# Moving the start-up loads and scale chains of a graph layer with expert routing, and its bias from a matmul to a vector add

## Chip, cores and metric

The kernel runs on one core of a Trainium2 chip. The metric is the device time of one execution in microseconds (us), the median over the runs.

## What is computed

The input is x (6250 nodes, 512 features, float32), a list of 106,250 edges sorted by destination, and the weights of one graph layer and of one layer of 16 experts. Cut to what matters:

```python
def _L0_gnn_ref(x, src, dst, W_self, b_self, W_neigh, gamma, beta, alpha):
    deg = segment_sum(ones_like(src), dst, N)
    agg = segment_sum(x[src], dst, N)
    neigh = agg * (1.0 / maximum(deg, 1.0))[:, None]
    h = x @ W_self + b_self + neigh @ W_neigh
    h = layernorm(h) * gamma + beta
    h = where(h >= 0, h, alpha * h)
    return h + x
x = x + _L0_gnn_ref(_layernorm(x), src, dst, ...)
x = x + _L0_ffn_ref(_layernorm(x), gate_weight, w1, w2)   # top 2 of 16 experts, mean over each expert's tokens
```

## The kernel before

Nodes are worked in 49 tiles of 128 (the last, the tail, has 106). All matmuls of float32 data are made of two float16 parts of each operand, a high and a low one: `split_mm` issues three products for each of four chunks, 12 matmuls in all.

**Stage one, tiles in order.** SyncE loads x tiles into a ring of eight (`load_x`). VectorE takes their statistics (`stats_of`), four tiles form a quarter, and `scales_of(q)` turns the quarter's means and variances into the scale and bias of the normalization. For quarters 0 and 1 all of that is on VectorE; from quarter 2 on VectorE only aggregates (counter `a_mv`) and GpSimd computes the chain (counter `a_stat`). ScalarE normalizes (`normal`), TensorE transposes (`turn_x`), ScalarE casts the high part and VectorE subtracts for the low one (`turned_high`, `turned_low`), and TensorE multiplies by the neighbour weights (`project`, through `split_mm`). The result is stored as a table row pair of float16 (`neigh_high`, `neigh_low`, `store_table`). The instruction order on ScalarE is written out by hand: for each tile i the cast of tile i, the normalization of i+2, the high part of the projection of i-1. Between tiles VectorE and TensorE do side work given by tables of tile numbers (`lists`): the edge lists (`passed_tiles` at tile 1, `turns`, `hits` and so on), and at tiles 17 to 25 the maxima of the self weights (`self_maxima`), their scale (`powers`), the bias parts (`self_bias`) and low parts (`self_low`).

The neighbour weights are scaled by a power of two drawn from their largest magnitude (`powers(1, 7, 0, 1)`), then cast in one ScalarE instruction (line 684) and lowered in one VectorE instruction (line 1300). All weights are loaded from ScalarE's queue in the first microseconds, the edge lists and then x from SyncE's.

**Stage two, edges in order.** The edges are cut into 208 groups of 4 x 128. For each, GpSimd issues four indirect gathers of 128 table rows (2 KB each) into a ring of four groups (line 617); it reuses a place in the ring when TensorE's step counter `c_step` says that the group is spent. A step (`step`) multiplies one-hot matrices made by ScalarE with the gathered rows and adds into one of two PSUM banks; there are 257 steps, one more at each tile's border. Beside the first 45 steps TensorE also computes one tile's self product each (`side`): a bias matmul of `kilo` and `bparts` (line 934), then 12 products; four more of these stand ahead of them. When a tile's steps are done, VectorE evicts it in `gnn`: it scales and adds the self product (line 1344), clears the bank, which frees it for TensorE (line 1346), then takes the moments, normalizes, applies the slope, adds the residual, and normalizes again into two float16 halves (lines 1349 to 1369). In 16 of the tiles it also takes a maximum of expert weights, and in 16 others it splits them (lines 1379 and 1382).

**Stage three** routes tokens on VectorE, gathers them by expert, runs the experts, and mixes and stores the output.

## Time and profile before

| | |
|---|---|
| median of three timed runs | 1692.03 us (1685.09 to 1693.57) |
| the profiled execution's own time | 1686.77 us |
| its span, first to last instruction | 1685.0 us |
| mean granted TensorE clock | 0.887 of full speed |
| TensorE matmuls busy | 1217.9 us (72%) |
| VectorE busy | 1028.5 us (61%) |
| GpSimd busy | 992.6 us (59%) |
| ScalarE busy | 886.9 us (53%) |

The busy shares are averages over stages with different limits, so they don't say what an edit is worth: that is read from the stage in which the edited work runs. A line number such as L617 is that of the kernel before; PE is TensorE, PEld its weight load, DVE VectorE, ACT ScalarE, POOL GpSimd, SP SyncE. A number in brackets behind an instruction is how long its engine stood idle before it, and what ended that.

### The profile page before, as it was taken

What the parts mean: (1) busy time and instruction counts of PE and PEld (TensorE: products, weight loads), DVE (VectorE), ACT (ScalarE), POOL (GpSimd) and SP (SyncE); (2) the same over time, 40 slices, a digit from 0 to 9 for tenths busy, and PEclk for the clock granted to TensorE, in tenths of its full rate; (3) what the DMA queues carried; (4) which work ended last, traced back from release to release, by engine and by line L of the source; (5) the groups of instructions that cost most, each with busy time, mean ns of one, the idle gap of its engine ahead of it and who ended that gap; (6) DMA issues with size and microseconds to landing.
All of it is one profiled execution on the core that took longest, in us unless ns stands there. A gap on an engine that the chain in (4) does not pass through costs nothing.

```text
span 1685.0 us, 37100 instructions
## 1 busy us (share of the span) xinstructions
PE 1217.9 (72%) x7688; PEld 644.5 (38%) x7696; DVE 1028.5 (61%) x2918; ACT 886.9 (53%) x1932; POOL 992.6 (59%) x1193
## 2 busy tenths in 40 slices
PE   4989899999665555665565546666677159999876
PEld 2545444444322222222222222234444146777612
DVE  6676235546666665657566655655658966666626
ACT  3455445555644444444444444446667838888402
POOL 2223277676777777777777777777776025555200
PEclk9999999999988888778878897799999669999885
DMA  5445277777888887888888888778877526666547
GB/s 194 141 139 166 108 219 252 243 250 225 265 265 268 264 245 237 280 260 296 261 281 279 285 279 275 240 237 249 246 233 219 216 80 201 199 200 205 192 167 275
DMA packets 141638, 384.99 MB, mean 228 GB/s; under 512 B 22911, under 2 KB 23041, under 8 KB 141509
## 3 DMA queue, kind: packets, MB, share of 16 engines
q0 software_dynamic: 75840, 248.18, 48.9%
q1 hardware_dynamic: 62392, 130.43, 21.8%
q10 hardware_dynamic: 3276, 4.97, 0.9%
q8 instruction: 43, 0.70, 0.2%
q14 instruction: 87, 0.70, 0.1%
...
## 4 chain that ended last, share of the span: by engine, by line
PE 39%; POOL 24%; issue 16%; DVE 9%; DMA 7%; POOLq 2%; SPq 2%; ACT 1%; DVEq 0%; ACTq 0%
POOL work L617 24%; PE ps L861 13%; PE ps L960 10%; PE ps L1053 6%; DMA work<-table,work 4%; PE ps L1064 3%; PE ps L1055 3%; POOLq L612 2%; PE ps L1113 1%; SPq L525 1%; DMA work<-in_w_t 1%; DMA work<-in_x 1%; PE ps L907 1%; DVE slots L1515 1%; PE ps L934 1%
## 5 line engine op out<-in xcount | busy, mean ns | idle before, releaser
L617 POOL DMA_INDIRECT work<-table,work x832 | 828.4, 996 | 295.6 <-issue 239.8
L960 PE MATMUL ps<-work 128*128 x2056 | 574.6, 431 | 345.0 <-DMA work<-table,work 329.5
L960 PEld LDWEIGHTS ps<-work 128*128 128x128 f16 x2056 | 216.4, 106 | 589.9 <-issue 445.3
L715 ACT ACTIVATE work<-work,ones 128x512 f16<-128x512 f16 x259 | 185.3, 715 | 325.7 <-PE ps L963 325.2
L709 ACT ACTIVATE work<-iota_row,work 128x128 f16<-128x128 f32 x1040 | 331.3, 390 | 31.6 <-ACT work L715 23.9
L861 PE MATMUL ps<-wparts,slots 128*128 128x512 f16 x1176 | 274.1, 383 | 12.2 <-DVE slots L1251 12.2
L1339 DVE TENSOR_SCALAR inv<-ps 128x1 f32 (+2 forms) x49 | 7.7, 158 | 336.6 <-PE ps L963 331.9
L633 POOL DMA_INDIRECT slots<-x_d,betab x114 | 107.8, 946 | 161.8 <-PE ps L1064 83.9
L861 PEld LDWEIGHTS ps<-wparts,slots 128*128 128x128 f16 x1176 | 115.8, 99 | 139.8 <-DVE slots L1251 14.7
L1053 PE MATMUL ps<-work,wparts 128*128 x456 | 156.1, 382 | 2.2 <-ACT wparts L801 2.0
L801 ACT COPY wparts<-ps 128x1024 f16<-128x1024 f16 x114 | 115.3, 1012 | 59.8 <-PE ps L1064 59.1
L1055 PE MATMUL ps<-work,wparts 128*128 x456 | 125.0, 274 | 0.0
L1553 DVE TENSOR_REDUCE work<-ps 128x256 f32<-128x512 f32 x114 | 78.7, 691 | 41.4 <-PE ps L1055 40.3
L963 PEld LDWEIGHTS ps<-onesh,work 128*128 128x128 f16 x1028 | 68.3, 102 | 76.5 <-issue 28.5
L729 ACT COPY wparts<-ps 128x1024 f16<-128x1024 f16 (+1 forms) x49 | 49.4, 1009 | 81.3 <-PE ps L976 80.2
L721 ACT ACTIVATE slots<-ps,wscale 128x512 f32<-128x512 f32 (+1 forms) x49 | 33.6, 686 | 103.0 <-PE ps L861 103.0
L1545 DVE TENSOR_TENSOR slots<-slots,work 128x256 f32 x114 | 52.8, 464 | 39.2 <-issue 24.5
L1064 PE MATMUL ps<-identh,slots 128*128 128x128 f16 x912 | 70.8, 221 | 5.1 <-DMA slots<-x_d,betab 5.1
L1064 PEld LDWEIGHTS ps<-identh,slots 128*128 128x128 f16 x912 | 61.4, 99 | 20.3 <-issue 5.3
L681 ACT ACTIVATE work<-ps 128x512 f16<-128x512 f32 (+1 forms) x49 | 29.2, 596 | 75.7 <-PE ps L861 75.7
L587 POOL TENSOR_SCALAR var<-mv 128x4 f32<-128x4 f32 x11 | 2.5, 228 | 108.3 <-DVE mv L1233 108.3
L963 PE MATMUL ps<-onesh,work 128*128 128x1 f16 x1028 | 64.1, 166 | 0.0
...
## 6 DMA issues: line engine op xcount, KB each, us to landing
...
```

The costliest lines, as they stand in the source:

```text
L617: pool.indirect_dma_start(out=gath[:, g % GRING, w, :], out_offset=None, in_=table[:, :], in_offset=bass.IndirectOffsetOnAxis(ap=idx_all[: ...
L633: pool.indirect_dma_start(out=xf[:, b, :], out_offset=None, in_=x2_d[:, :], in_offset=bass.IndirectOffsetOnAxis(ap=idx2[:, k:k + 1], axis= ...
L709: last = act.activation(away[:, par, w, :], iota_row[:, :], ACT.Abs, bias=negd[:, ds(GT * k + w, 1)])
L715: act.activation(hot[:, slot, :, :], away[:, slot % 2, :, :], ACT.Relu, bias=ones[:, 0:1], scale=-1.0).then_inc(c_hot, 1)
L801: act.copy(xft[:, b, :, :, :], chunks16(bank16(6 + n % 2), P)).then_inc(f_xt, 1)
L861: last = pe.matmul(to, left(a, c), right(w, c), start=start and c == 0 and a == 0 and w == 0, stop=c == n - 1 and a == 1)
L960: pe.matmul(ps[:, ds(bank, 1), :], hot[:, s, w, :], gath_row[:, ds(at + (2 * w + half) * D, D)].unsqueeze(1), start=False, stop=True, skip ...
L963: last = pe.matmul(ps[:, BANKS:2 * BANKS, 0:1][:, ds(bank, 1), 0], hot[:, s, w, :], onesh[:, :], start=False, stop=True, skip_group_check= ...
L1053: pe.matmul(ps[:, HBANK + b, :].rearrange("p (u a n) -> p u a n", u=1, a=2), xft[:, b, 0, c, :], both, start=c == 0, stop=c == CHUNKS - 1, ...
L1055: last = pe.matmul(ps[:, HBANK + b, FF:2 * FF].unsqueeze(1), xft[:, b, 1, c, :], high, start=False, stop=c == CHUNKS - 1, skip_group_check ...
L1064: last = pe.transpose(bank16(6 + n % 2)[:, j * P:(j + 1) * P], xf[:, b, j * P:(j + 1) * P], identh[:, :])
L1553: dve.tensor_reduce(hid[:, b, :], ps[:, HBANK + b, :].rearrange("p (a n) -> p n a", a=2), X, ALU.add).then_inc(f_pre, 1)
```

## The change

1. SyncE issues the first four x tiles ahead of the edge lists. VectorE takes their statistics before it turns to the neighbour weights, and quarters 0 and 1 get their scale chain on GpSimd as the others do.
2. The six loads that are not the neighbour weights (self and gate weights, bias, alpha, gamma, beta) move from ScalarE's queue to GpSimd's, behind the scale chain of quarter 0. The four spare fills and the store to the first row of x2 now stand behind them.
3. ScalarE normalizes tiles 0 and 1 before it casts the neighbour weights, and casts them in four chunks; VectorE lowers each chunk as it comes, and the first projection waits chunk by chunk.
4. The bias matmul of each self product goes, with the bias's maximum and its preparation in two float16 parts. VectorE adds the float32 bias to each finished tile in `gnn`, behind the clear that frees the bank and ahead of the moments.
5. The bias stays in SBUF for longer, at a place that expert 14's weights take later; so expert 14's load moves from the first group of the last loads to the late one, which then has four loads instead of three.

```diff
@@ -185,11 +183,12 @@
         xin = cut(UNROLL * D, 0).rearrange("p (b n) -> p b n", b=UNROLL)
         xs = cut(HALF * D).rearrange("p (b n) -> p b n", b=HALF)
         tb = cut(HALF * D).bitcast(f16).rearrange("p (b n) -> p b n", b=HALF)
-        RAW_AT = place[0]
+        BSELF_AT = 14464
         wst = cut((2 * D + EXPERTS) * CHUNKS)
         ws, wn, gw = (wst[:, a * CHUNKS:b * CHUNKS].rearrange("p (c n) -> p c n", c=CHUNKS)
                       for a, b in ((0, D), (D, 2 * D), (2 * D, 2 * D + EXPERTS)))
-        bself = cut(D)
+        assert place[0] <= BSELF_AT
+        bself = cut(D, BSELF_AT)
         TABLES = GROUPS * GT + (STEPS + 3) * GT + STEPS + GROUP_CHUNKS * P + TILES
         assert place[0] <= WORK - TABLES
         idx_all = cut(GROUPS * GT, WORK - TABLES).bitcast(i32)
...
@@ -373,6 +369,14 @@
                 sp.sem_inc(d_st[b], 16)
             sp.sem_inc(v_st, 16)
             sp.sem_inc(d_x2st, 16)
+            def load_x(i):
+                r = rows_of(i)
+                if i >= UNROLL:
+                    sp.wait_ge(a_xs, i - UNROLL + 1)
+                sp.dma_start(xin[0:r, i % UNROLL, :], x[i * P:i * P + r, :]).then_inc(a_x[i % UNROLL], 16)
+
+            for i in range(HALF):
+                load_x(i)
             early = (GROUP_CHUNKS - 1) * P * GE_EDGES
             whole = (EDGES - early) // GE_EDGES
             half = whole - whole % 16
@@ -389,18 +393,12 @@
                              a[early + whole * GE_EDGES:EDGES].rearrange("(p e) -> p e", p=1)).then_inc(s_edge, 16)
 
 
-            def load_x(i):
-                r = rows_of(i)
-                if i >= UNROLL:
-                    sp.wait_ge(a_xs, i - UNROLL + 1)
-                sp.dma_start(xin[0:r, i % UNROLL, :], x[i * P:i * P + r, :]).then_inc(a_x[i % UNROLL], 16)
-
             def store_table(i):
                 r = rows_of(i)
                 sp.wait_ge(a_z, i + 1)
                 sp.dma_start(table[i * P:i * P + r, :], tb[0:r, i % HALF, :]).then_inc(a_st[i % HALF], 16)
 
-            for i in range(UNROLL):
+            for i in range(HALF, UNROLL):
                 load_x(i)
             for i in range(TILES + 2):
                 if i + UNROLL < TILES:
...
@@ -485,13 +483,13 @@
             sp.wait_ge(c_step, HOTS + STEPS)
             sp.wait_ge(c_away, STEPS + 3)
             sp.wait_ge(c_hot, STEPS + 2)
-            for e in list(range(9)) + list(range(12, EXPERTS)):
+            for e in list(range(9)) + [12, 13, 15]:
                 load_w1s(e)
             store_x1(LAST, 0, TAIL)
             store_x2(LAST, 0, TAIL)
             for b in range(2):
                 sp.wait_ge(d_st[b], 16 * (1 + len(range(b, TILES, 2))))
-            for e in range(9, 12):
+            for e in (9, 10, 11, 14):
                 load_w1s(e)
 
             def load_x1(i, rows):
...
@@ -572,18 +569,12 @@
                                base=-1, pattern=[[1, EXPERTS + 1]], channel_multiplier=-1).then_inc(s_const, 1)
 
 
-            pool.wait_ge(s_const, 2)
-            for n, s in enumerate(c_g):
-                pool.dma_start(spare[16 * n:16 * (n + 1), :],
-                               zero[16 * n:16 * (n + 1), :].bitcast(f16)).then_inc(s, 16 * GT)
-            pool.dma_start(x2_d[0:1, :], zero[0:1, :].bitcast(f16)).then_inc(d_zero, 16)
-
             def scales_of(q):
                 tiles = part_tiles(q)
                 n, r, c0 = len(tiles), slice(0, rows_of(tiles[-1])), q % 2 * HALF
                 at, c = slice(q * HALF, q * HALF + n), slice(c0, c0 + n)
                 v, g, f = (a[:, HALF:2 * HALF] for a in (var, guess, fix))
-                pool.wait_ge(a_mv, q - 1)
+                pool.wait_ge(a_mv, q + 1)
                 ln.link(pool.tensor_scalar(v, mv[:, c0:c0 + HALF, 1], EPS, None, ALU.add))
                 ln.link(pool.tensor_scalar(g.bitcast(i32), v.bitcast(i32), -0.5, float(0x5f3759df), ALU.mult, ALU.add))
                 for _ in range(3):
@@ -594,11 +585,26 @@
                 pool.tensor_scalar(rstd1[r, at], g[r, 0:n], 1.0, None, ALU.add)
                 ln.link(pool.tensor_tensor(nmr[r, at], mv[r, c, 0], g[r, 0:n], ALU.mult))
                 ln.link(pool.tensor_scalar(nmr[r, at], nmr[r, at], -1.0, None, ALU.mult))
-                pool.wait_ge(a_xs, HALF * (q - 1))
+                if q >= 2:
+                    pool.wait_ge(a_xs, HALF * (q - 1))
                 pool.tensor_scalar(gs[r, c], g[r, 0:n], SCALE, None, ALU.mult)
                 pool.tensor_scalar(gb[r, c], nmr[r, at], SCALE, None, ALU.mult).then_inc(a_stat, 1)
 
-            for q in range(2, PARTS):
+            scales_of(0)
+
+            for to, what in ((ws[:, :, :], w_self.rearrange("(c p) n -> p c n", p=P)),
+                             (gw[:, :, :], gate_t.rearrange("(c p) n -> p c n", p=P)),
+                             (bself[:, :], b_self.to_broadcast([P, D])), (alphab[:, :], alpha.to_broadcast([P, 1])),
+                             (gammab[:, :], gamma.to_broadcast([P, D])), (betab[:, :], beta.to_broadcast([P, D]))):
+                pool.dma_start(to, what).then_inc(s_w, 16)
+
+            pool.wait_ge(s_const, 2)
+            for n, s in enumerate(c_g):
+                pool.dma_start(spare[16 * n:16 * (n + 1), :],
+                               zero[16 * n:16 * (n + 1), :].bitcast(f16)).then_inc(s, 16 * GT)
+            pool.dma_start(x2_d[0:1, :], zero[0:1, :].bitcast(f16)).then_inc(d_zero, 16)
+
+            for q in range(1, PARTS):
                 scales_of(q)
 
             for b in range(HALF):
@@ -650,11 +656,6 @@
             act.sem_inc(g_rts, CREDIT)
             act.sem_inc(c_self, 2)
             act.dma_start(wn[:, :, :], w_neigh.rearrange("(c p) n -> p c n", p=P)).then_inc(s_wn, 16)
-            for to, what in ((ws[:, :, :], w_self.rearrange("(c p) n -> p c n", p=P)),
-                             (gw[:, :, :], gate_t.rearrange("(c p) n -> p c n", p=P)),
-                             (bself[:, :], b_self.to_broadcast([P, D])), (alphab[:, :], alpha.to_broadcast([P, 1])),
-                             (gammab[:, :], gamma.to_broadcast([P, D])), (betab[:, :], beta.to_broadcast([P, D]))):
-                act.dma_start(to, what).then_inc(s_w, 16)
 
 
             def normal(i):
@@ -680,10 +681,11 @@
                     act.wait_ge(a_st[i % HALF], 16 * (i // HALF))
                 act.activation(tb[0:r, i % HALF, 0:D], ps[0:r, 2 + i % 2, :], ACT.Copy, scale=2.0 ** -ZBITS).then_inc(a_zhi, 1)
 
-            act.wait_ge(w_scale, 1)
-            act.activation(wnp[:, 0, :, :], wn[:, :, :], ACT.Copy, scale=wscale[:, 0:1]).then_inc(w_hi, 1)
             normal(0)
             normal(1)
+            act.wait_ge(w_scale, 1)
+            for c in range(CHUNKS):
+                act.activation(wnp[:, 0, c, :], wn[:, c, :], ACT.Copy, scale=wscale[:, 0:1]).then_inc(w_hi, 1)
             for i in range(TILES):
                 if i == TILES - LIST_TILES:
                     act.wait_ge(b_done, 1)
@@ -912,13 +914,17 @@
                 pe.wait_ge(a_lo, i + 1)
                 if i >= 2:
                     pe.wait_ge(a_z, i - 1)
-                split_mm(ps[0:r, 2 + i % 2, :], lambda a, c: xt[:, i, a, c, 0:r], lambda w, c: wnp[:, w, c, :],
-                         CHUNKS).then_inc(a_mm, 1)
+
+                def weights(w, c):
+                    if i == 0 and w == 0:
+                        pe.wait_ge(w_lo, c + 1)
+                    return wnp[:, w, c, :]
+
+                split_mm(ps[0:r, 2 + i % 2, :], lambda a, c: xt[:, i, a, c, 0:r], weights, CHUNKS).then_inc(a_mm, 1)
 
             pe.wait_ge(s_const, 1)
             powers(1, wmax[:, 0:1], 7, 1)
             turn_x(0)
-            pe.wait_ge(w_lo, 1)
             for i in range(TILES):
                 if i + 1 < TILES:
                     turn_x(i + 1)
@@ -931,12 +937,10 @@
                 rows = rows_of(i)
                 pe.wait_ge(c_self, i + 1)
                 to = ps[0:rows, 5 + i % 2, :]
-                pe.matmul(to, kilo[:, 0:rows], bparts[:, :], start=True, stop=False)
-                split_mm(to, lambda a, c: xt[:, i, a, c, 0:rows], lambda w, c: wsp[:, w, c, :], CHUNKS,
-                         start=False).then_inc(c_mm, 1)
+                split_mm(to, lambda a, c: xt[:, i, a, c, 0:rows], lambda w, c: wsp[:, w, c, :], CHUNKS).then_inc(c_mm, 1)
 
             pe.wait_ge(b_done, 1)
-            pe.wait_ge(w_lo, 2)
+            pe.wait_ge(w_lo, CHUNKS + 1)
             pe.wait_ge(s_const, 2)
             side(0)
             pe.wait_ge(a_z, TILES)
@@ -1229,21 +1233,10 @@
                 n, r, c0 = len(tiles), slice(0, rows_of(tiles[-1])), q % 2 * HALF
                 if q >= 2:
                     dve.wait_ge(a_stat, q - 1)
-                    for m in range(n):
-                        last = dve.bn_aggr(mv[r, c0 + m, :], stats[r, m, :])
-                    last.then_inc(a_mv, 1)
-                    dve.wait_ge(a_mv, q - 1)
-                    return
                 for m in range(n):
-                    last = dve.bn_aggr(mv[r, m, :], stats[r, m, :])
-                ln.link(last)
-                ln.link(dve.tensor_scalar(var[:, 0:HALF], mv[:, 0:HALF, 1], EPS, None, ALU.add))
-                rstd_chain(ln, HALF)
-                at = slice(q * HALF, q * HALF + n)
-                dve.tensor_scalar(rstd1[r, at], guess[r, 0:n], 1.0, None, ALU.add)
-                ln.link(dve.scalar_tensor_tensor(nmr[r, at], mv[r, 0:n, 0], -1.0, guess[r, 0:n], ALU.mult, ALU.mult))
-                dve.tensor_scalar(gs[r, c0:c0 + n], guess[r, 0:n], SCALE, None, ALU.mult)
-                dve.tensor_scalar(gb[r, c0:c0 + n], nmr[r, at], SCALE, None, ALU.mult).then_inc(a_stat, 1)
+                    last = dve.bn_aggr(mv[r, c0 + m, :], stats[r, m, :])
+                last.then_inc(a_mv, 1)
+                dve.wait_ge(a_mv, q + 1)
 
             def turned_low(i):
                 r = rows_of(i)
@@ -1260,24 +1253,16 @@
             def self_maxima():
                 dve.wait_ge(s_w, 16 * 6)
                 dve.tensor_reduce(wmax[:, 1:2], flat(ws[:, :, :]), X, ALU.max, apply_absolute_value=True)
-                dve.tensor_reduce(wmax[:, 2:3], flat(gw[:, :, :]), X, ALU.max, apply_absolute_value=True)
-                ln.link(dve.tensor_reduce(wmax[:, 3:4], bself[:, :], X, ALU.max, apply_absolute_value=True))
-                dve.tensor_tensor(wmax[:, 1:2], wmax[:, 1:2], wmax[:, 3:4], ALU.max).then_inc(w_max, 1)
+                dve.tensor_reduce(wmax[:, 2:3], flat(gw[:, :, :]), X, ALU.max, apply_absolute_value=True).then_inc(w_max, 1)
 
             def self_bias():
                 dve.wait_ge(w_scale, 2)
                 dve.tensor_scalar(alpha_less[:, :], alphab[:, :], 1.0, None, ALU.subtract)
                 dve.tensor_scalar(valid[:, :], iota_p[:, 0:1], float(TAIL), None, ALU.is_lt)
                 dve.tensor_scalar(nowhere[:, :], iota_p[:, 0:1], float(TAIL), float(NOWHERE), ALU.is_ge, ALU.mult)
-                ln.link(dve.tensor_scalar(bhi[:, :], bself[:, :], wscale[:, 1:2], None, ALU.mult))
-                dve.tensor_scalar(bsel[:, 0:1], iota_p[:, 0:1], 0.0, None, ALU.is_equal)
-                dve.tensor_scalar(bsel[:, 1:2], iota_p[:, 0:1], 1.0, None, ALU.is_equal)
-                ln.link(dve.scalar_tensor_tensor(blo[:, :], bself[:, :], wscale[:, 1:2], bhi[:, :], ALU.mult, ALU.subtract))
-                ln.link(dve.tensor_scalar(blo[:, :], blo[:, :], bsel[:, 1:2], None, ALU.mult))
-                dve.scalar_tensor_tensor(bparts[:, :], bhi[:, :], bsel[:, 0:1], blo[:, :], ALU.mult, ALU.add)
 
             def self_low():
-                dve.wait_ge(w_hi, 2)
+                dve.wait_ge(w_hi, CHUNKS + 1)
                 dve.scalar_tensor_tensor(wsp[:, 1, :, :], ws[:, :, :], wscale[:, 1:2], wsp[:, 0, :, :], ALU.mult, ALU.subtract)
                 dve.scalar_tensor_tensor(gwp[:, 1, :, :], gw[:, :, :], wscale[:, 2:3], gwp[:, 0, :, :],
                                          ALU.mult, ALU.subtract).then_inc(w_lo, 1)
@@ -1286,19 +1271,20 @@
                           SELF_AT[4]: self_low})
 
             dve.wait_ge(s_const, 1)
+            for i in part_tiles(0):
+                last = stats_of(i)
+            ln.link(last)
+            dve.nop(nofuse=True)
+            scales_of(0)
             dve.wait_ge(s_wn, 16)
             dve.tensor_reduce(wmax[:, 0:1], flat(wn[:, :, :]), X, ALU.max, apply_absolute_value=True).then_inc(w_max, 1)
             powers(1, 7, 0, 1)
             dve.wait_ge(w_scale, 1)
             dve.tensor_scalar(wscale[:, 8:9], wscale[:, 4:5], 2.0 ** ZBITS, None, ALU.mult)
-            for i in part_tiles(0):
-                last = stats_of(i)
-            ln.link(last)
-            dve.nop(nofuse=True)
-            scales_of(0)
-            dve.wait_ge(w_hi, 1)
-            dve.scalar_tensor_tensor(wnp[:, 1, :, :], wn[:, :, :], wscale[:, 0:1], wnp[:, 0, :, :],
-                                     ALU.mult, ALU.subtract).then_inc(w_lo, 1)
+            for c in range(CHUNKS):
+                dve.wait_ge(w_hi, c + 1)
+                dve.scalar_tensor_tensor(wnp[:, 1, c, :], wn[:, c, :], wscale[:, 0:1], wnp[:, 0, c, :],
+                                         ALU.mult, ALU.subtract).then_inc(w_lo, 1)
             for i in range(TILES):
                 turned_low(i)
                 for j in (HALF + 2 * i, HALF + 2 * i + 1) if i < HALF // 2 else ():
@@ -1323,7 +1309,7 @@
             count = ln.n
 
 
-            LINKS = 38
+            LINKS = 39
 
             def gnn(it, b, rows=P, maxima=False, split=False, tail=False):
                 j, bank = HALF * it + b, (b + 1) % BANKS
@@ -1344,6 +1330,8 @@
                 ln.link(dve.scalar_tensor_tensor(slot, ps[r, bank, :].unsqueeze(1), share, slot, ALU.mult, ALU.add))
                 dve.memset(ps[:, BANKS + bank, 0:1], 0.0)
                 dve.memset(ps[:, bank, :], 0.0).then_inc(c_ev, 1)
+                ln.link(dve.tensor_tensor(slot, slot, bself[r, :].unsqueeze(1), ALU.add))
+                dve.nop(nofuse=True)
 
                 def moments(of):
                     ln.link(dve.bn_stats(stats[r, 0, :], of))
```

## Rows read from the trace of the kernel before

**Rows 1.** The page's chain that ended last: shares of the span by engine.
```profile
PE 39%; POOL 24%; issue 16%; DVE 9%; DMA 7%; POOLq 2%; SPq 2%; ACT 1%; DVEq 0%; ACTq 0%
```

**Rows 2.** Busy time by stretch: stretch, length, each engine's busy us (instructions), granted clock, DMA.
```profile
0.00:10.00 10.00, 0.00 (x0) 0.01 (x1) 2.20 (x2) 1.28 (x1) 8.86 (x35) 1.00 0.73 245
40.00:190.00 150.00, 140.01 (x731) 75.48 (x730) 98.88 (x204) 79.85 (x132) 41.04 (x203) 1.00 0.42 140
215.00:427.00 212.00, 212.00 (x1146) 98.92 (x1145) 109.79 (x355) 113.40 (x277) 150.41 (x155) 1.00 0.76 240
427.00:1262.00 835.00, 504.27 (x3069) 249.43 (x3068) 518.64 (x1678) 421.25 (x1025) 640.01 (x641) 0.85 0.84 262
1262.00:1375.00 113.00, 48.98 (x552) 33.91 (x551) 95.97 (x292) 75.58 (x186) 31.25 (x32) 0.76 0.51 172
```

**Rows 3.** GpSimd's waits from 204 to 427 us: total, times, longest.
```profile
POOL work L617 <- PE ps L963: 17.7, 10, 2.9
```

**Rows 4.** GpSimd's groups by line, 427 to 1262 us: busy, mean ns, idle before.
```profile
L617 POOL DMA_INDIRECT work<-table,work x641 | 641.0, 1000 | 195.3 <-issue 185.9 <-PE ps L963 9.4
```

**Rows 5.** The chain in order of time, 217.6 to 222.3 us: start, us, what.
```profile
217.80 2.59 PE ps L861 x12
220.39 1.73 PE ps L960 x8
...
222.20 0.24 PE ps L934
```

**Rows 6.** The timeline of the first 44 us: start, us, engine, line, operation.
```profile
7.69 2.20 POOL L577 DMA_DIRECT2D spare<-zero  x4 [0.34 <-POOL shift L571]
...
19.96 0.16 DVE L1246 TENSOR_SCALAR gb<-nmr 128x4 f32<-128x4 f32 x1
20.15 1.52 ACT L665 ACTIVATE work<-work,gb,gs 128x512 f32<-128x512 f32 x2 [5.04 <-DVE gb L1246]
...
23.54 3.33 PE L861 MATMUL ps<-wparts,slots 128*128 128x512 f16 x12
...
34.24 4.45 PE L861 MATMUL ps<-wparts,slots 128*128 128x512 f16 x12 [3.90 <-DVE slots L1251]
...
38.34 0.25 POOL L587 TENSOR_SCALAR var<-mv 128x4 f32<-128x4 f32 x1 [27.97 <-DVE mv L1233]
...
40.26 2.75 PE L861 MATMUL ps<-wparts,slots 128*128 128x512 f16 x12
...
43.38 0.22 POOL L599 TENSOR_SCALAR gb<-nmr 128x4 f32<-128x4 f32 x1
```

**Rows 7.** The timeline around the bias's maximum and its preparation, 90 to 112 us.
```profile
93.85 0.68 DVE L1264 TENSOR_REDUCE wmax<-work 128x1 f32<-128x512 f32 x1
...
95.38 2.76 PE L861 MATMUL ps<-wparts,slots 128*128 128x512 f16 x12 [1.66 <-DVE slots L1251]
...
108.50 0.48 DVE L1272 TENSOR_SCALAR slots<-work,wscale 128x512 f16<-128x512 f32 x1
...
110.32 0.75 DVE L1277 SCALAR_TENSOR_TENSOR bparts<-slots 128x512 f16<-128x512 f16 x1
...
111.73 0.60 PE L861 MATMUL ps<-wparts,slots 128*128 128x512 f16 x2 [1.21 <-DVE slots L1251]
```

**Rows 8.** The timeline of gathers beside VectorE's work on one tile, 776 to 792 us.
```profile
779.78 1.40 POOL L617 DMA_INDIRECT work<-table,work  x1 [0.30 <-issue]
...
788.40 0.69 DVE L1369 TENSOR_TENSOR slots<-work,slots 128x512 f32 x1
789.05 0.95 POOL L617 DMA_INDIRECT work<-table,work  x1 [0.30 <-issue]
789.90 1.28 DVE L1382 SCALAR_TENSOR_TENSOR work<-work,wscale 128x1024 f16<-128x1024 f32 x1
790.30 1.70 POOL L617 DMA_INDIRECT work<-table,work  x1 [0.30 <-issue]
```

**Rows 9.** VectorE's timeline behind the last steps.
```profile
1312.05 0.75 DVE L1344 SCALAR_TENSOR_TENSOR slots<-ps,inv,slots 106x512 f32<-106x512 f32 x1
```

10 lines of the change are left out of this document (2 added, 8 removed).

## Prediction

> **What bounds the kernel now.** I read the chain that ended last first, for which engines carry the end, and see four kinds of time in it: TensorE 39%, GpSimd 24% (nearly all of it gathers of line 617), issue 16%, VectorE 9% [rows 1]. Shares over the whole span do not price an edit, so I cut the span by stage next [rows 2]. From 40 to 190 us, the projection of all 49 tiles, TensorE is busy 140.0 of 150 us. From 215 to 427, the steps that carry a self product, it is busy all 212 us at the full granted clock (1.00, the 2.4 GHz level). From 427 to 1262 it is busy 60%; there GpSimd issues one gather after another. From 1262 to 1375 VectorE is busy 96.0 of 113 us. So four different engines' work is worth money in four places, and each part of the change must be priced where it lands.
>
> GpSimd's waits decide how far the second stage passes on to the third. Between 204 and 427 it waits 17.7 us for TensorE's counts, beside the 0.3 us of issue that each gather has anyway [rows 3]. After 427 it hardly waits for TensorE (9.4 us, no more than those 0.3 us each): 641 gathers of 1.00 us and 0.30 us between them fill the 835 us [rows 4]. Each gather costs 1.25 us when undisturbed (0.95 and 0.30 [rows 8]). So the gathers are the bound after 427 and TensorE before it, with 17.7 us of slack in GpSimd.
>
> **Part 1, bias matmul out of TensorE.** One step with a self product is, in the chain, 12 products in 2.59 us, 8 in 1.73, 4 small ones in the 0.08 behind them and the bias matmul in 0.24: 4.64 us [rows 5]. The chain has no other engine in it there, so the matmul is removed from the path in full. Products of this width take 2.59 / 12 = 0.216 us each, the bias line 0.22 to 0.24; I take 0.22. Of 49, the first two run before the gathers can start (TensorE waits for the table anyway) and are worth nothing; 47 x 0.22 = 10.3 us. TensorE reaches the last self product 10.3 us earlier, and GpSimd, released by its counts, follows as long as its slack of 17.7 us lasts: 7.4 us are left. Gain 10.3 us; bounds 8 (some of the slack lies where it cannot be used) and 10.8.
>
> **Part 2, bias preparation out of VectorE.** Two TensorE pauses of stage one end at VectorE: 1.66 us at 95.38 and 1.21 us at 111.73 [rows 7]. Ahead of the first, VectorE loses the maximum of the bias (line 1264, 0.68 us, and the small merge behind it: 0.7 us of pace). Ahead of the second it loses lines 1272 to 1277, from 108.50 to 111.07 (110.32 + 0.75), 2.5 us, more than the pause. Gain 0.7 + 1.2 = 1.9, say 2.0; bounds 1.2 and 2.3. What is late next is nothing: TensorE then runs at its own pace.
>
> **Part 3, the start.** Today the scale chain of quarter 0 ends at about 20.1 (19.96 + 0.16), ScalarE normalizes two tiles in 1.52 us right behind it, and the first product starts at 23.54 [rows 6]. The first ten us moved 245 GB/s [rows 2]. Four x tiles and w_neigh are 2.1 MB, and with them first in their two queues, and some of the edge lists beside them, I put the fourth tile at 9.5 us (bounds: 8, if edges do not share, and 11.5, if all do). Then 0.7 us of statistics and 0.4 of aggregates: 10.6. The chain on GpSimd costs what it costs for quarter 2, from 38.34 to 43.60 = 5.3 us, against 2.9 on VectorE: 15.9. The maximum (2.3) and the powers (about 3, from 10.1 to 13.1 today) end at 15.9 too, on other engines. ScalarE then does two normalizations (0.8 each), four quarter casts (0.6 each, an estimate above a quarter of the 2.0 us of the whole) and the cast of tile 0 (0.6): 20.5; VectorE's low part (0.7) gives a first product at 21.2, a gain of 2.3.
>
> The third projection (tile 2) waited for VectorE, which did quarter 1's chain (2.9 us) and the edge work first: TensorE stood 3.90 us and the product then took 4.45 us where the next ones take 2.75 [rows 6]. Without that chain it starts near 29.8, 4.4 us sooner. But quarter 1's scales now stand in GpSimd's queue behind the moved steps: six weight loads and then the four spare fills and the x2 row, which it is moved ahead of for quarter 0 only. The four fills took 2.20 us, 0.55 each for 16 rows ([rows 6]; 2.7 us with the x2 row's); a 128-row gather costs 1.0 us [rows 4]. w_self and the gate matrix have 512 rows each, the other four 128: between 6 x 0.55 = 3.3 us and 12 x 1.0 = 12 us. I take 9.8, by rows rather than by instruction count. GpSimd is free at 15.9 + 9.8 + 2.7 = 28.4 (bounds 21.9 and 30.6), while quarter 1's aggregates are ready at about 24.8; its chain ends at 33.7. Who waits for it: ScalarE's normalization of tile 4, and behind that instruction in ScalarE's order the high part of tile 1's projection and the cast of tile 3, 0.8 + 0.6 + 0.6 us, and then VectorE's 0.7: tile 3's product starts at 36.4 against 40.26 today [rows 6], 3.9 us gained. With GpSimd free early it is 5.8, with the upper bound 1.7. I take 4.0. The weights themselves are wanted only at tile 17, near 91 us, so their landing later costs nothing; quarter 2 on are computed on GpSimd already. The edge lists are issued 1.8 us later and are wanted behind tile 1; nothing waits.
>
> **Part 4, the bias add on VectorE.** A 128x512 add of this form takes 0.69 us (line 1369 [rows 8]), 0.7 with its link. While steps run it lies behind the clear that frees the bank, so TensorE does not wait, and VectorE is idle a third of stage three: no direct cost. Behind the last steps VectorE alone carries three tiles' evictions (line 1344 starts three times in that stretch, for the last time at 1312.05 for the tail [rows 9]): 3 x 0.7 = 2.1 us lost.
>
> The unseen price is what the add does to the gathers it overlaps. In [rows 8] the gather beside line 1382 took 1.70 us instead of 0.95, one beside line 1356 took 1.40, one beside line 1369 0.95. Over stage three the 641 gathers cost 641.0 us where 0.95 each would be 609: 32 us more. Sixteen uses of line 1382 at some 0.8 take 13 of that, 19 us are left for 39 tiles, 0.5 us a tile, which five adds or multiplies with two SBUF operands share. I take 0.1 us for the new one: 39 x 0.1 = 4 us lost. Bounds: 0 and 0.2, 8 us.
>
> The Trainium skill (SBUF — State Buffer, "SBUF: two separate sides") speaks against this part: a VectorE instruction with two SBUF inputs and a GpSimd one that reads SBUF exclude each other, for the whole instruction. By that, a gather that comes due at a random moment of the 1.25 us period waits 0.69 x 0.69 / 2.5 = 0.19 us on average, 7.4 us in all, and the sum below would be 3.4 us smaller. The trace shows both a long gather and an undisturbed one beside such instructions, so it is not decided there.
>
> **Sum.** -10.3 - 2.0 - 4.0 + 2.1 + 4.0 = -10.2 us. The profiled execution took 1686.8 us (span 1685.0), so its counterpart is 1676.6; it is 5.2 us under the median of the three timed runs, 1692.0, and on that footing I predict 1681.8 us. Half a per cent, 8.5 us, is about what a measurement here tells from no change.
>
> **Rivals.**
> *The start is swallowed by GpSimd's queue.* Loads that cost 1 us per 128 rows or more, a late fourth tile, or a table switch put quarter 1's scales past 38 us; the gain of part 3 is then nil and the time 1685.8. For it: nothing in the trace is a GpSimd load of 512 rows. Against it: VectorE's 2.9 us are really gone. Chance 0.14, inside half a per cent.
> *The add stalls the gathers.* If it stalls them as line 1382 does (0.75 us for 1.28 us of work, so 0.41 for 0.69), the loss is 39 x 0.41 = 16 us instead of 4 and the net is +1.8: 1693.8; if each add blocks a gather in full (0.69), 27 us and +12.8: 1704.8. It turns the sign at 14.2 / 39 = 0.36 us per add. Against it: the five like instructions per tile share 0.5 us today. Chance 0.13, some 0.08 of it beyond half a per cent.
> *The gathers bind from the first step.* Then the shorter steps only add waits to TensorE, and the bias matmuls give nothing: net +0.1, 1692.1. Against it: 17.7 us of GpSimd waits. Chance 0.05.
> *More than forecast.* GpSimd issues loads at 0.55 us, TensorE keeps its clock through the first 40 us, and the add is free: start 7, net -17, 1675. Chance 0.10.
>
> **Numbers.** The forecast itself has 0.58, with its own range of -5 to -14 (1687 to 1678), of which about 0.42 lies beyond 8.5 us. Faster: 0.42 + 0.10 + a little = 0.54; slower 0.08; same 0.38. The range: from the good case, 1675, and some run-to-run spread below it (the three runs span 8.5 us), to the point where the add's price eats the gain: 1672 to 1694.
>
> **What would show it.** Right: first product near 21 us; tile 3's near 36; no pause at lines 1251 behind the maxima and behind self_bias; steps of 4.42 us with self products; GpSimd's waits for TensorE before the last self product down from 17.7 to some 7 us; mean gather after it at most 1.01 us; the stretch from the last gather to the first expert product longer by 2 us. Wrong: a gather mean of 1.03 or more (part 4), a GpSimd load above 3 us each for the wide ones (part 3), or steps that wait for the gathers while self products run (part 1).

## The result, and the profile after

The changed kernel takes 1705.15 us (median of 6 runs, 1702.05 to 1709.22), the kernel before 1690.61 (6 runs, 1685.09 to 1693.57) on the same chip. The ratio is 1.010, its 95% interval 1.0082 to 1.0118: slower by 14.5 us, where 10.2 faster was forecast. The profiled execution spans 1700.3 us, 15.3 more than the one of before. The profiled executions of both lie under their medians, by 3.8 us (1686.8) and by 3.1 (1702.05), so the trace and the medians agree here. Below, those of e1, e2, e3 and e13 are the longest of their runs, so gains read from these traces come out a few us smaller than gains of medians, and the loss in e3 larger.

The windows of the changed kernel, cut as in [rows 2] (length, then PE, PEld, DVE, ACT and POOL busy us, granted clock, DMA share, GB/s):

```profile
0.00:10.00 10.00, 0.00 (x0) 0.01 (x1) 2.80 (x6) 1.28 (x1) 6.40 (x29) 1.00 0.78 279
40.00:190.00 150.00, 141.55 (x737) 76.26 (x735) 95.87 (x196) 78.91 (x131) 39.13 (x194) 1.00 0.42 140
215.00:427.00 212.00, 205.18 (x1124) 96.24 (x1122) 129.05 (x405) 124.30 (x308) 162.18 (x161) 1.00 0.81 251
427.00:1262.00 835.00, 502.74 (x2940) 244.50 (x2940) 522.05 (x1645) 399.40 (x970) 646.13 (x621) 0.82 0.82 255
1262.00:1375.00 113.00, 51.15 (x539) 32.49 (x541) 94.67 (x305) 83.71 (x204) 41.85 (x39) 0.77 0.58 190
```

Read the third and the fourth line against [rows 2]. In the same 212 us GpSimd does 161 operations, not 155: the steps with a self product became faster. In the same 835 us it does 621, not 641, and is busier with them. The gain is made in one stage and lost in the next. The page's chain shows GpSimd at 26% where it was 24% [rows 1]:

```profile
PE 39%; POOL 26%; issue 16%; DMA 8%; DVE 6%; POOLq 2%; SPq 1%; ACT 1%; DVEq 0%; ACTq 0%
```

GpSimd's groups by line, first of the whole span, then of 427 to 1262 us (busy, mean ns of one, idle before):

```profile
L623 POOL DMA_INDIRECT work<-table,work x832 | 863.0, 1037 | 282.0 <-issue 238.2 <-DMA table<-work 27.8 <-PE ps L967 16.0
...
L623 POOL DMA_INDIRECT work<-table,work x621 | 647.0, 1042 | 189.2 <-issue 177.3 <-PE ps L967 11.9
```

The mean gather went from 1000 ns [rows 4] to 1042. The prediction named 1.03 as the sign that part 4 is wrong.

Sharper than shares is the start of one and the same gather, counted from the first, in both traces. The table gives the start in another kernel minus the start before, in us:

| gather | start before | changed | without the add (e1) |
|---|---|---|---|
| 0 | 204.03 | -5.80 | -3.74 |
| 160 | 424.04 | -15.33 | -13.25 |
| 300 | 604.50 | -9.62 | -12.59 |
| 500 | 867.99 | -2.05 | -13.69 |
| 700 | 1130.41 | +5.91 | -14.68 |
| 831 | 1299.11 | +15.05 | -13.35 |

The first three parts bring the gathers forward by 15.3 us. From gather 160 on, 30.4 us are lost over 671 gathers, some in every stretch. In the same stretch the gathers are busy 702.3 us, not 671.8: 30.5 more, which come out one for one. Ahead of gather 160 they are busy 4.1 us longer (160.7 and 156.6), and that is not seen in the starts: GpSimd's slack pays for it. And the span ends 15.3 later, as the last gather does. So the question for the experiments is part 4 alone, and why it costs 30 us and not 4.

### The profile page after: what moved, and what is told of

Read it like the earlier page. It is cut to its first block, busy times and chain, and to the rows that moved or that the text cites. A ratio compares the mean times of both kernels' runs of the same rounds, so it can differ in the third digit from the quotient of the medians.

```text
span 1700.3 us, 37145 instructions
## 1 busy us (share of the span) xinstructions
PE 1223.6 (72%) x7639; PEld 644.8 (38%) x7647; DVE 1055.5 (62%) x2930; ACT 887.5 (52%) x1935; POOL 1039.3 (61%) x1236
## 4 chain that ended last, share of the span: by engine, by line
PE 39%; POOL 26%; issue 16%; DMA 8%; DVE 6%; POOLq 2%; SPq 1%; ACT 1%; DVEq 0%; ACTq 0%
POOL work L623 25%; PE ps L863 13%; PE ps L964 11%; PE ps L1057 6%; DMA work<-table,work 5%; PE ps L1068 3%; PE ps L1059 3%; POOLq L618 2%; PE ps L1117 1%; SPq L523 1%; DMA work<-in_w_t 1%; PE ps L909 1%; DMA work<-in_x 1%; DVE slots L1503 1%; DVE slots L1469 1%
## 5 line engine op out<-in xcount | busy, mean ns | idle before, releaser
L623 POOL DMA_INDIRECT work<-table,work x832 | 863.0, 1037 | 282.0 <-issue 238.2
L964 PE MATMUL ps<-work 128*128 x2056 | 591.4, 440 | 359.2 <-DMA work<-table,work 340.1
L964 PEld LDWEIGHTS ps<-work 128*128 128x128 f16 x2056 | 219.9, 108 | 614.6 <-issue 477.0
L863 PE MATMUL ps<-wparts,slots 128*128 128x512 f16 x1176 | 274.3, 384 | 17.3 <-DVE slots L1244 11.2
L797 ACT ACTIVATE work<-work,wscale 128x256 f32<-128x256 f32 x114 | 58.1, 510 | 8.0 <-DVE work L1541 7.8
```

The source lines that it names most:

```text
L623: pool.indirect_dma_start(out=gath[:, g % GRING, w, :], out_offset=None, in_=table[:, :], in_offset=bass.IndirectOffsetOnAxis(ap=idx_all[: ...
L863: last = pe.matmul(to, left(a, c), right(w, c), start=start and c == 0 and a == 0 and w == 0, stop=c == n - 1 and a == 1)
L964: pe.matmul(ps[:, ds(bank, 1), :], hot[:, s, w, :], gath_row[:, ds(at + (2 * w + half) * D, D)].unsqueeze(1), start=False, stop=True, skip ...
```

## The beginning, up to the last self product

The timeline of the changed kernel's first 40 us, against [rows 6]:

```profile
15.47 0.22 POOL L591 TENSOR_SCALAR gb<-nmr 128x4 f32<-128x4 f32 x1
...
15.75 1.01 POOL L599 DMA_DIRECT2D work<-in_w_self  x1
16.78 0.79 POOL L599 DMA_DIRECT2D work<-in_gate_t  x1
17.54 0.57 POOL L599 DMA_DIRECT2D work<-in_b_self  x1
...
21.29 5.15 PE L863 MATMUL ps<-wparts,slots 128*128 128x512 f16 x12 [2.72 <-DVE slots L1244]
...
31.66 2.76 PE L863 MATMUL ps<-wparts,slots 128*128 128x512 f16 x12 [1.76 <-DVE slots L1244]
...
35.98 2.75 PE L863 MATMUL ps<-wparts,slots 128*128 128x512 f16 x12
```

The first product starts at 21.29 (forecast 21.2) and tile 3's at 35.98 (forecast 36.4, 40.26 before). The six loads cost GpSimd 1.01, 0.79 and four times 0.57 or 0.56, some 4.0 us, where I took 9.8 between bounds of 3.3 and 12. One thing I had not priced: the first 12 products now take 5.15 us, 0.43 each, where they took 3.33 before [rows 6], so of the 2.25 us of the earlier start 0.4 are left at that product's end. The traces show only two paces for such a product: 0.43 us from one start to the next, which is 1.2 columns per ns, and 0.216, which is 2.4. By that TensorE ran at the lower of its two clock levels (1.2 and 2.4 GHz), although the granted clock of the stretch reads 1.00 in both traces. In the kernel before, three of the twelve came at the slow pace, right behind the transposes; in the changed kernel eleven did, and TensorE had stood idle for 2.72 us just ahead of them. The product of tile 2 in the kernel before, behind 3.90 us of idle time, also ran at the slow pace for its last eight, and took 4.45 us [rows 6].

The delay passes on through VectorE, which waits for the first product's result ahead of the edge work:

```profile
27.18 0.69 DVE L1250 SCALAR_TENSOR_TENSOR work<-ps,work 128x512 f16<-128x512 f32 x1 [2.48 <-ACT work L682]
```

So tile 2's product starts at 31.66 and not at the 29.8 of the forecast.

The two pauses of [rows 7], 1.66 and 1.21 us, in the changed kernel's timeline:

```profile
90.33 2.76 PE L863 MATMUL ps<-wparts,slots 128*128 128x512 f16 x12 [0.87 <-DVE slots L1244]
...
106.01 2.76 PE L863 MATMUL ps<-wparts,slots 128*128 128x512 f16 x12 [0.55 <-DVE slots L1244]
```

They are 0.79 and 0.66 shorter, 1.45 us in all of the forecast 2.0. They did not vanish. Ahead of the first, VectorE still takes the maximum of the self weights, 2.27 us. At the second, VectorE itself stands:

```profile
105.26 0.69 DVE L1244 TENSOR_TENSOR slots<-ps,slots 128x512 f16<-128x512 f32 x1 [1.73 <-ACT slots L674]
```

It waits 1.73 us for ScalarE's cast of the tile, which stands behind ScalarE's casts of the self and gate weights (1.99 and 0.34 us). The prediction had put what is late next at nothing. The chain in order of time in a step with a self product:

```profile
214.14 1.73 PE ps L964 x8
215.86 0.08 PE ps L967 x4
215.94 2.61 PE ps L863 x12
```

That is the 4.42 us per step of the forecast, without the fourth piece of [rows 5]. GpSimd's waits for TensorE between 204 and 420 us are down from the 17.7 of [rows 3] (from the first gather at 198 us to gather 160 they are 2.9):

```profile
POOL work L623 <- PE ps L967: 3.2, 7, 1.4
```

Without the add (e1 and e2 below) they are 9.7 and 10.7 up to gather 160: the stalls of the add use up the rest. Up to here the prediction's sum was 16.3 us and the trace shows 15.3.

## Experiments: is it the add?

Four kernels on one chip, where the kernel before took 1689.51 us.

**e1_no_add** is the changed kernel with the add taken out, so that the bias is left out of the result.

```
-                ln.link(dve.tensor_tensor(slot, slot, bself[r, :].unsqueeze(1), ALU.add))
-                dve.nop(nofuse=True)
```

> The changed kernel with the bias add left out of every tile (its output lacks the bias); all else as changed. Theory A (the add, which reads two SBUF operands, holds up the gathers it overlaps): the 832 gathers, 863.0 us busy in the changed kernel, fall back to some 830, the lead of 15.3 us that the kernel has at its 160th gather is kept to the end, and the time is about 1705 - 34 - 2 = 1669 us. Theory B (the add's 0.7 us of VectorE time per tile is late for something else, a transfer or a bank): also about 1669, so this run doesn't part A from B. Theory C (the moved loads, the new place of the bias or the earlier start make the gathers slower, not the add): 1703, gathers still above 860 us.

Measured: 1672.06 us (1669.87 to 1673.67), ratio 0.9896 (0.9873 to 0.9919). Gathers 827.5 us in all, mean 995 ns. The gain is 17.5 us by the medians and 13.1 by the profiled spans (1685.0 to 1671.9), and the first three parts were forecast to give 16.3. Nearly all of the loss goes with one instruction of 0.67 us per tile.

**e2_psum_add** keeps the add and changes where its operand lies: the eviction writes its result back into the PSUM bank, the add reads PSUM and the bias and writes the slot, and the clear comes behind both.

```
-                ln.link(dve.scalar_tensor_tensor(slot, ps[r, bank, :].unsqueeze(1), share, slot, ALU.mult, ALU.add))
+                acc = ps[r, bank, :]
+                ln.link(dve.scalar_tensor_tensor(acc.unsqueeze(1), acc.unsqueeze(1), share, slot, ALU.mult, ALU.add))
+                ln.link(dve.tensor_tensor(slot, acc.unsqueeze(1), bself[r, :].unsqueeze(1), ALU.add))
                 dve.memset(ps[:, BANKS + bank, 0:1], 0.0)
                 dve.memset(ps[:, bank, :], 0.0).then_inc(c_ev, 1)
-                ln.link(dve.tensor_tensor(slot, slot, bself[r, :].unsqueeze(1), ALU.add))
                 dve.nop(nofuse=True)
```

> The changed kernel with the same add, but the tile is evicted into its PSUM bank first and the add reads PSUM and one SBUF operand; the bank is cleared behind it. Same VectorE time, the bank free 0.75 us later, output as the reference. Theory A: the gathers cost some 830 us, time about 1669 + 2 = 1671 us. Theory B: as the changed kernel, 1705 us or a little more. Theory C: 1705 us.

Measured: 1672.57 us (1668.68 to 1674.20), ratio 0.9896 (0.9871 to 0.9921). Gathers 825.9 us, mean 993. The same add, done just as often and as long (0.69 us, 0.67 in the changed kernel), is free. Two rows of its timeline show why:

```profile
431.59 0.69 DVE L1332 TENSOR_TENSOR slots<-ps,work 128x512 f32 x1
431.83 0.95 POOL L623 DMA_INDIRECT work<-table,work  x1 [0.30 <-issue]
```

A gather that becomes due in the middle of the add takes its plain 0.95 us. So do all 29 gathers that start during such an add (at most 0.95 us), and the 18 that an add meets in their first half microsecond. In the changed kernel 27 gathers start during the add, and 23 of them are stretched.

**e3_before_add** goes the other way: the kernel before, with an add of a tile of zeros at the same place, behind the clear.

```
+                ln.link(dve.tensor_tensor(slot, slot, zero[r, :].unsqueeze(1), ALU.add))
+                dve.nop(nofuse=True)
```

> The kernel before with one instruction more per tile: a tile of zeros added at the place of the bias add, two SBUF operands, output unchanged. Theory A: gathers from 828 to about 863 us busy and the time 1690.6 + 30 to 36 = 1721 to 1727 us, less what GpSimd's 17.7 us of slack before 427 us hides (some 3). Theory B: the same. Theory C: only the 2.1 us behind the last steps, 1693 us.

Measured: 1711.61 us (1710.65 to 1715.67), ratio 1.0133 (1.011 to 1.0156). Gathers 859.8 us, mean 1033. The last gather starts 27.9 us later than before, the profiled span is 28.9 us longer (1713.9), the median 22.1. The direction was as expected and the size was not: the median lies 6 us under the least expected, 1721 less 3 for the slack. Between the changed kernel and e1 the add costs 28.4 us by the profiled spans, as here, and 33.1 by the medians. Whether the price is really lower in the kernel before stays open.

**e4_start_only** keeps the start (part 3), puts the bias matmul and its preparation back, and has no add in the tiles.

> The changed loads, scale chains and weight casts alone: the bias is again prepared and added by a matmul as before, and no add stands in the tiles. Theories A and B: the gathers begin some 4 us sooner (the 5.8 us of the changed kernel less 2 for the bias preparation) and cost what they did: 1686.5 us. Theory C: the gathers still cost 860 us or more and the time is above 1700 us.

Measured: 1686.11 us (1683.73 to 1688.95), ratio 0.9981 (0.9967 to 0.9996). The first gather starts 4.5 us earlier, the last 2.6, and the time is 3.4 us lower; part 3 was forecast at 4.0. Against the changed kernel's first gather (5.8 earlier) 1.3 are left for part 2. That difference is too small to rest on: e1, e2, e13 and e14 do the same work up to the first gather as the changed kernel, and it starts 3.7, 6.3, 7.1 and 5.8 us earlier in them.

## Experiments: why 30 us, and not 16?

The prediction's rival had priced a stall like that of line 1382: 16 us. To see who stalls whom I put every gather that took over 0.95 us down to the VectorE instruction that overlapped its beginning. In all traces a gather stalled by an instruction with two tensors in SBUF ends 0.81 to 0.83 us behind that instruction's end, with a handful of exceptions. The sum over the 832 gathers, in us, with the number of tiles in brackets (line numbers of the changed kernel; those of before in the text):

| | before | changed |
|---|---|---|
| the new add, L1333 | - | 17.3 (40 of 49) |
| first multiply of the normalization, L1344 (1356) | 4.3 (15) | 15.3 (37) |
| L1350 (1362) | 6.4 (14) | 12.4 (27) |
| L1357 (1369) | 3.8 (24) | 6.7 (36) |
| L1370 (1382) | 12.8 (16) | 13.2 (16) |
| all, with the rest | 40.9 | 75.3 |

The add's own stalls are 17.3 us: 0.43 per stalled add, where the rival had 0.41. But half of the loss, 17.1 us, stands at instructions that were there before. The changed kernel's timeline of one tile shows how:

```profile
433.71 0.67 DVE L1333 TENSOR_TENSOR slots<-slots,work 128x512 f32 x1
433.71 1.49 POOL L623 DMA_INDIRECT work<-table,work  x1 [0.30 <-issue]
435.50 0.95 POOL L623 DMA_INDIRECT work<-table,work  x1 [0.30 <-issue]
436.76 0.95 POOL L623 DMA_INDIRECT work<-table,work  x1 [0.30 <-issue]
437.82 0.75 DVE L1344 SCALAR_TENSOR_TENSOR work<-slots,norm,gammab 128x512 f32<-128x512 f32 x1
438.01 1.38 POOL L623 DMA_INDIRECT work<-table,work  x1 [0.30 <-issue]
```

The stalled gather ends at 435.20, 0.82 us behind the add's end, and sets the rhythm of the next ones: one each 1.25 us, due at 435.50, 436.76, 438.01. The small instructions between the add and line 1344 take a fixed time, so line 1344 starts 4.11 us behind the add (433.71 to 437.82; 4.10 us in 36 of the 49 tiles, at most 4.36 in the others), just ahead of the gather due at 438.01, and stalls it: 1.38. The stall ties the gathers to VectorE's chain: in 39 of the 40 tiles with a stalling add the next gather starts 1.79 us behind the add's start. The chain's fixed lengths then decide what is hit next. The tie is not all of it: line 1344 stalls a gather in 31 of those 40 tiles, and also in 6 of the 8 in which the add stalled none beside it. Where the add falls in the middle of a gather nothing happens:

```profile
519.76 0.67 DVE L1333 TENSOR_TENSOR slots<-slots,work 128x512 f32 x1
520.45 0.95 POOL L623 DMA_INDIRECT work<-table,work  x1 [0.30 <-issue]
```

If that reading is right, the knock-on can be taken away without touching the add. The rival reading is that line 1344 stalls more simply because VectorE has one instruction more.

**e14_shift** is the changed kernel with three narrow instructions (0.53 us together) between the first moments and line 1344, and so with more work on VectorE.

```
+                for n in range(3):
+                    ln.link(dve.tensor_scalar(norm1[r, 5 + n:6 + n], guess[r, 0:1], 1.0, None, ALU.mult))
```

> The changed kernel with three narrow instructions of some 0.2 us between the first moments and line 1344. In the changed kernel line 1344 starts 4.1 us behind the add, nearly always 1.05 us into the 1.25 us period of the gathers, and stretches the next gather by 0.43 us. Phase theory: 0.6 us later it starts 0.4 us into a period, where such an instruction stopped no gather in the trace of before; its 15.3 us of stalls all but vanish, the gathers fall from 863 to some 848 us and the time to 1705 - 15 + 2 = 1692 us, 1685 to 1697. Rival (the stall follows the instruction, not its place in the period): 1707 us.

Measured: 1692.68 us (1688.91 to 1696.01), ratio 1.002 (1.0005 to 1.0035) to the kernel before on that chip (1688.97). Gathers 845.4 us, mean 1016, where the changed kernel has 863.0. Its timeline:

```profile
550.80 0.95 POOL L623 DMA_INDIRECT work<-table,work  x1 [0.30 <-issue]
551.01 0.75 DVE L1346 SCALAR_TENSOR_TENSOR work<-slots,norm,gammab 128x512 f32<-128x512 f32 x1
552.05 1.32 POOL L623 DMA_INDIRECT work<-table,work  x1 [0.30 <-issue]
```

The same multiply (now line 1346, 4.66 us behind the add) starts 0.2 us into a gather and ends before the next is due: both the gather at 550.80 and the multiply pass untouched. Of the stalls put down to it 0.4 us are left, in 2 tiles, and those of the add remain (15.9 us, 29 tiles). Line 1347, the next one, has 9.1 us where it had 1.8 (line 1345 of the changed kernel), and the gather at 552.05 is one of its; line 1352 has 8.1 where it had 12.4 (line 1350). Adding 0.53 us of work per tile gave back 17.6 us of gather time and about 0.8% of the kernel. That is phase (the place in the gathers' period), not load.

**e12_half_add** is the kernel before with a zeros add of half the width (256 elements), behind the clear. **e11_add_later** is the kernel before with a full add in SBUF (the tile of zeros to itself), whose result nobody needs, in the middle of the second moments. Both ran on a chip where the kernel before took 1690.08.

```
+                ln.link(dve.tensor_tensor(slot[:, :, 0:D // 2], slot[:, :, 0:D // 2], zero[r, 0:D // 2].unsqueeze(1), ALU.add))
...
+                    if of is x1_of[0]:
+                        ln.link(dve.tensor_tensor(x2f[r, :], zero[r, :], zero[r, :], ALU.add))
```

> The kernel before with a half-width add of zeros behind the clear, on a chip where the kernel before takes 1690 us. If the price goes with the overlap: near 1700 us, gathers some 845 us. If each such instruction costs a fixed amount: 1711 us, gathers near 860 us.

> The kernel before with the unneeded add of two SBUF tiles in the middle of the second moments, on a chip where the kernel before takes 1690 us. Theory A1 (any such add stops a gather when it meets its start): 1705 to 1715 us, gathers near 855 us busy. Theory A2 (the place behind the step's end is special, by what it does to the multiplications that follow): under 1703 us, gathers under 848 us.

Measured: e12 1704.53 us (1704.33 to 1704.53, 3 runs), ratio 1.0084 (1.0056 to 1.0111), gathers 846.3 us. e11 1688.34 us (1685.76 to 1694.40), ratio 0.9997 (0.9978 to 1.0016), gathers 831.5 us. Half the width has about half the direct stalls of e3 (10.4 us against 19.7) and nearly all of its knock-on at the first multiply (11.8 against 14.8, 35 tiles in both). A full add further down costs nothing that can be measured: it stalls gathers for 7.7 us in 25 tiles, but all stalls together are 43.9 us against 40.9, since others fall. So the price of an instruction of this form is not a property of the instruction: nothing measurable in one place and 22 us in another, for the same 0.67 to 0.69 us per tile.

**e13_psum_all** takes the cure as far as it goes: the changed kernel with all wide two-tensor instructions of a tile reading one operand from the PSUM bank, which is cleared at the tile's end.

```
-                moments(slot)
-                ln.link(dve.scalar_tensor_tensor(hb[r, :].unsqueeze(1), slot, mean, gammab[r, :].unsqueeze(1), ALU.subtract, ALU.mult))
-                ln.link(dve.scalar_tensor_tensor(hb[r, :], hb[r, :], guess[r, 0:1], betab[r, :], ALU.mult, ALU.add))
+                moments(acc)
+                ln.link(dve.scalar_tensor_tensor(acc, acc, mean, gammab[r, :], ALU.subtract, ALU.mult))
+                ln.link(dve.scalar_tensor_tensor(acc, acc, guess[r, 0:1], betab[r, :], ALU.mult, ALU.add))
...
+                dve.wait_ge(d_x2, 2 + j + 1)
+                dve.memset(ps[:, BANKS + bank, 0:1], 0.0)
+                dve.memset(ps[:, bank, :], 0.0).then_inc(c_ev, 1)
```

> Every wide two-tensor instruction of the eviction on a PSUM operand, on a chip where the kernel before takes 1690 us. Theory A: 30 us less in the gathers than with only the add moved (795.6 against 825.9 us busy on the other chip), 1643 to 1656 us. Rival (the bank comes free late and TensorE waits for it): above 1675 us.

Measured: 1647.83 us (1647.09 to 1652.03), ratio 0.9746 (0.9717 to 0.9775). Its groups of GpSimd, and a stretch of its timeline:

```profile
L623 POOL DMA_INDIRECT work<-table,work x832 | 801.6, 964 | 290.5 <-issue 235.2 <-DMA table<-work 27.8 <-PE ps L967 27.5
```

```profile
515.48 0.94 POOL L623 DMA_INDIRECT work<-table,work  x1 [0.30 <-issue]
515.54 0.76 DVE L1343 SCALAR_TENSOR_TENSOR ps<-ps,norm,gammab 128x512 f32<-128x512 f32 x1
516.73 0.94 POOL L623 DMA_INDIRECT work<-table,work  x1 [0.30 <-PE ps L967]
```

Of 40.9 us of stalls in the kernel before, some 15 are left, 10.8 of them at the weights' split (line 1372, 16 instructions), which still reads SBUF alone. The last gather starts 38.7 us earlier than before. The rival of the expectation, a TensorE that waits for the bank, is not seen: the trace has no wait of TensorE for a bank's clear. Its one long wait for VectorE, 17.3 us, is behind the last step, for the tail's finished tile, and the kernel before has it too (13.9 us; 14.2 in the changed kernel).

**Where the gathers don't bind.** The kernels of e13, e11 and e12 ran first, as e5 to e7, on a chip where the kernel before took 1978.22 us, and, as e8 to e10, on another with 1979.41.

> The changed kernel with the add's cure spread over the tile: all intermediate results of a tile's eviction stay in its PSUM bank, so that each of the six wide VectorE instructions on two tensors (the bias add and lines 1344, 1345, 1347, 1350 and 1357 of the changed kernel) has one operand in PSUM, and the bank is cleared at the end of the tile's work instead of at its start. Theory A (only two SBUF operands, or a two-port single-operand instruction, stop a gather): excess of the 832 gathers over 0.95 us falls from some 36 us (run with the add from PSUM) to that of line 1370 (14 us) and the single-operand ones (about 5), time about 1672.6 - 17 = 1656 us. Rival: the bank, which now comes free some 13 us after its last step instead of 2, makes TensorE wait for it in every second tile; then steps start late and the time is above 1675 us.

> The kernel before with an unneeded add of two SBUF tiles (512 wide, into a scratch tile) in the middle of the second moments, among narrow instructions, instead of behind the clear. Theory A1 (each add stops a gather when their starts fall together, wherever it stands): about the same cost as at the place behind the clear, direct stalls near 0.3 to 0.4 us per add and 15 to 25 us in all, time 1705 to 1715 us. Theory A2 (the place behind the step's end is special, since gathers and evictions are released by the same counter, or since the add sets the phase for the two multiplications 3 us later): less than half of it, under 1700 us.

> The kernel before with a half-width add of zeros (256 elements, some 0.4 us) behind the clear, in place of the full one of 0.69 us. If the price is the overlap with the gather's start, the direct stall goes with the window in which they meet, 0.6 us instead of 0.9, squared: 0.14 us per add instead of 0.32, some 7 us direct; with the same knock-on as the full one the time is near 1700 us. If any such instruction costs a fixed amount, it is as the full one, 1711 us.

> The same kernel as in the last run with every wide two-tensor instruction of the eviction on a PSUM operand, on a chip where the kernel before takes some 1690 us. Its gathers were 795.6 us busy there against 825.9 with only the add moved. Theory A: issue of gathers is the bound here, so the 30 us come off in full where GpSimd isn't waiting: 1672.6 - 17 to 30 = 1643 to 1656 us. Rival (the bank comes free late and TensorE waits for it): above 1675 us.

> The kernel before with the unneeded add of two SBUF tiles in the middle of the second moments. Theory A1 (any such add stops a gather when it meets its start): 1705 to 1715 us, gathers near 855 us busy. Theory A2 (the place behind the step's end is special): under 1700 us, gathers under 845 us; on the other chip they were 831.6 us, which speaks for A2.

> The kernel before with a half-width add of zeros behind the clear. If the price goes with the overlap: near 1700 us, gathers some 845 us. If each such instruction costs a fixed amount: 1711 us, gathers near 860 us.

| | time | ratio (95%) | gathers, us |
|---|---|---|---|
| e5_psum_all | 1989.77 | 1.0053 (1.0027 to 1.008) | 795.6 |
| e6_add_later | 1975.36 | 1.0004 (0.9973 to 1.0036) | 831.6 |
| e7_half_add | 1974.68 | 0.9974 (0.9944 to 1.0004) | 828.6 |
| e8_psum_all | 1987.24 | 1.0052 (1.0015 to 1.009) | 795.4 |
| e9_add_later | 1971.38 | 0.9946 (0.9905 to 0.9986) | 828.3 |
| e10_half_add | 1973.14 | 1.0025 (0.9976 to 1.0074) | 826.8 |

On these chips the times don't tell one theory from the other. The row of e9 shows the reason:

```profile
L617 POOL DMA_INDIRECT work<-table,work x832 | 828.3, 996 | 579.6 <-issue 224.7 <-PE ps L963 209.0 <-remote 118.1
```

GpSimd waits 209.0 us for TensorE's counts, where e11, the same kernel on another chip, waits 28.2. The gathers are no longer the bound, so shorter gathers are worth nothing there: e5 has 36.0 us less gather time than e6 and is 14 us slower. The longer hold of the PSUM banks does not explain that: TensorE's waits for a bank's clear are 10.7 us in e8 and none in e5. Why these chips run the steps more slowly is open: from 427 to 1262 us e9 issues 504 gathers, and the kernel before on the faster chip 641, with the granted clock at 0.74 where it is 0.85 in [rows 2]; from 40 to 190 us, in the projection, TensorE is as busy on both (140.1 and 140.0 us).

## Why the prediction was wrong

- **What bounds the kernel** was right: TensorE up to the last self product, the gathers after it. From gather 160 on, what was added to the gathers (30.5 us) came out in their starts (30.4) and at the end: +15.05 at the last gather, +15.3 at the end of the span.
- **Part 1**, 10.3 forecast. Between gather 0 and gather 160 the changed kernel gains 9.5 us (15.33 - 5.80), e1 the same 9.5, e2 9.9. Right, and inside its bounds of 8 to 10.8. Of GpSimd's slack 9.7 us are left in e1, where the forecast had 7.4; the 2.9 of the changed kernel are what the add's stalls leave of it.
- **Part 2**, 2.0 forecast, 1.45 in the pauses. Right in kind, a little too large: I took the second pause to close in full, and ScalarE's cast was late next.
- **Part 3**, 4.0 forecast: 4.3 at tile 3, 4.5 at the first gather in e4, 3.4 in e4's time. The size is right by luck, since two errors cancel: the loads cost 4.0 us rather than 9.8, for which the prediction itself had 5.8 us at tile 3, and the first product ran at 0.43 us per matmul, which put tile 2's product at 31.66 instead of 29.8.
- **Part 4, the three last adds**, 2.1 forecast. The tail's eviction moved by 15.8 us (1312.05 [rows 9] to 1327.83), the last gather by 15.05: 0.7 us ahead of it. The two adds that stand there do not hold it up in the changed kernel, where VectorE waits 3.40 us for TensorE between them and the tail. The tail's own add comes behind it: TensorE's work on the finished tail starts 14.40 us behind the eviction's start, not 13.57, 0.8 us more. That makes 1.6 us, and the span's end, 15.3 us later, shows less.
- **Part 4, what the add does to the gathers**, 4.0 forecast with a bound of 8, is the term that failed. It is 30.4 us by the gathers' starts, 34.6 by their busy time (828.4 to 863.0), of which 4.1 lie ahead of gather 160 in GpSimd's slack. The faulty step is "0.5 us a tile, which five adds or multiplies with two SBUF operands share. I take 0.1 us for the new one". The five stand at fixed distances in a chain, and what each costs goes by where it falls in the gathers' period: line 1356 stalled a gather in 15 tiles before, and the same multiply in 37 with the add ahead of it. An average over the five says nothing of a sixth. The new one is a stall of its own, 0.43 us in 40 of 49 tiles (17.3 us), and it moves the gathers to where the old ones hit them (17.1 us more). The rival that named the mechanism had the direct price nearly right at 0.41 and no knock-on in it; I gave it 0.13, and "against it" stood the same mistaken average. Its upper case, 1704.8, is where the time came out, but by another way: not each add blocking a gather in full.

The Trainium skill (SBUF — State Buffer, "SBUF: two separate sides") names the pair as it was found: a VectorE instruction with two SBUF inputs against a GpSimd one that reads SBUF, and e2 shows the condition, since the same add with a PSUM input costs nothing. The 0.19 us that I had worked out from it for gathers due at random moments was too small: 17.3 us over all 49 tiles is 0.35. What was wrong is the size of a stall. I had let a gather that already ran pass, but 17 adds that started 0.01 to 0.45 us into a gather took their plain 0.67 us each, and the gather took 0.55 to 0.99 longer. On that point the trace does not bear out the exclusion "for the whole instruction" as the prediction took it. The other 23 stretched the gather that came due by 0.06 to 0.54. Spread evenly over the 1.25 us these would make some 0.40 us per add, an estimate, so chance moments alone would have given about what was measured for the add itself.

What stays open: the size of the knock-on was not derived ahead of its run in general (only e14's was, from the changed kernel's phases), and e3's was overestimated by at least 6 us.
